# Routed blocks of 512 rows chosen after six batches, two shared tiles moved to the end, and a re-ordered opening

## The chip, the cores and the metric

One Trainium2 chip, one NeuronCore. The metric is the device time of one execution in microseconds; the median of 3 runs of the kernel before is 559.57 us (558.17 to 560.89). TensorE (PE) multiplies, VectorE (DVE), ScalarE (ACT) and GpSimd (POOL) work on elements, SyncE (SP) issues most DMAs. Each engine works through its own list of instructions in the order written, and semaphores order the engines among each other.

## What is computed

Eight batches of 512 tokens with 256 features, in float32: a pre-norm attention with one head and a causal mask, and then a pre-norm mixture of experts with one shared and eight routed experts, of which each token takes two.

```python
x = x + attn(layernorm(x), Wq, Wk, Wv)          # x: 8 x 512 x 256, causal, softmax(q k / 16)
h = layernorm(x)
shared = (silu(h @ sg.T) * (h @ su.T)) @ sd.T    # inner size 512
probs = sigmoid(h @ router.T + bias)             # 8 experts
scores, idx = top_k(probs, 2); scores /= scores.sum()
x = x + shared + sum over the two of scores * (silu(h @ gate[e]) * (h @ up[e])) @ down[e]
```

## The kernel before, in words

**Products.** Every operand is split into a float16 high and a low part, and each product is made of three passes, hi x hi, lo x hi and hi x lo (`PASSES`), summed in PSUM.

**First stage, attention.** The kernel goes through the eight batches. For each: statistics, normalising (`xn_normalise`, `xn_high`, `xn_low`), transposing by DMA, T = x (Wq Wk^T) and V products, scores, softmax, a DMA transpose of the probabilities, and PV; then the second norm, the logits, `route` and `weights` (the two experts of each token), `prefix` and `places` (the place of each token in the list of its expert), and `scatter`, which writes each token's normalised row and its scores to the lists in `rows` in HBM, one list of T + P rows for each expert. Batch 0 is transposed by TensorE instead (`first_transposes`, `first_xn_high`, `first_xn_low`).

The weights of the nine experts come in 36 pieces of 384 KB through two buffers: `w_load(g)` on SP (it waits for `w_low(g - 2)`), `w_scale(g)` and `w_high(g)` on ACT, `w_low(g)` on POOL, which counts up `w_lo`.

The shared expert is done in 16 tiles of 256 tokens (`SHARED`), two batches behind the attention: `shared_gate_up(t, half)` on TensorE; `tanh`, `split_h` on ACT and `ffn_gate`, `ffn_up`, `ffn_low` on DVE make the hidden values h; `shared_down(t)` multiplies them into the bank Y, and `add_shared(t)` on DVE adds Y to x1, the sum so far. A tile's half takes 24 matmuls of 256 columns, and so does its `down`. `gate_up` of the next tile's same half waits for `f_h` (gate and up have been read), `shared_down` for `f_lo` (h is complete) and for `y_read` (Y has been added), and the weight loads, the norms and this work share the queues in an order written out by hand. `out_base(b)` writes x1 of a batch to `out`.

**Second stage, routed experts.** The lists are cut into pieces by tables that DVE works out from the counts: 26 pieces of 256 rows ("pairs"), of which the first 18 are two halves of 9 blocks of 512 rows (`QUADS`, `table_of_quads`), 12 of 128 ("singles") and 7 of 64 ("halves"). `counts()` on TensorE sums the tokens of each expert over all eight batches, `cnt_mm` tells DVE, and `tab`, `tab2` and `tab3` tell the other engines that a table is written. Each step of a table is a small DVE operation on one partition. SP then reads row numbers into registers (`value_load`) and loads the rows with a transposing DMA (`load_pair_rows`, `load_single_rows`) and the scores (`load_pair_aux`). A pair runs like a shared tile, with the expert's number from a register; then ACT scales its result by the scores (`y_copy`) and POOL adds it to `out` in HBM, 128 rows at a time (`y_add`, `add_rows`), one addition at a time. All lists' first 128 rows are filled with padding at the start (`zero_rows`), and a piece may reach down into them.

**Around the stages.** TensorE ends the first stage with `shared_down(15)`, waits for `tab` and for all 36 weight pieces, and starts the first groups: pair 0, then (after `tab2`) single 0, pair 1, and so on. SP loads the first pairs only when all batches are scattered. The last group is pairs 24 and 25, its last half in chunks (`last_gate_up`, `down_parts`), so that the last addition starts early; the kernel ends with POOL's last addition.

## Time and profile before

| what | value |
|---|---|
| median of 3 runs | 559.57 us (558.17 to 560.89) |
| the profiled execution, first to last instruction | 555.3 us |
| TensorE busy | 518.0 us (93%), 4757 matmuls |
| DVE, ACT, POOL busy | 369.8 (67%), 301.0 (54%), 288.9 us (52%) |
| mean granted TensorE clock | 0.986 of full |
| DMA | 68.55 MB, mean 123 GB/s |

The busy share of TensorE is a share of time in which a matmul was under way; what counts for the end is where it was not, and what it then waited for. Start times and durations below are those of the profiled execution, in us from its first instruction. An operation's line is often that of a helper, so operations are told apart by tile and time. "xN" groups N like instructions that follow each other.

### The profile page before, as it was taken

What the parts mean: (1) busy time and instruction counts of PE and PEld (TensorE: products, weight loads), DVE (VectorE), ACT (ScalarE), POOL (GpSimd) and SP (SyncE); (2) the same over time, 40 slices, a digit from 0 to 9 for tenths busy, and PEclk for the clock granted to TensorE, in tenths of its full rate; (3) what the DMA queues carried; (4) which work ended last, traced back from release to release, by engine and by line L of the source; (5) the groups of instructions that cost most, each with busy time, mean ns of one, the idle gap of its engine ahead of it and who ended that gap; (6) DMA issues with size and microseconds to landing.
All of it is one profiled execution on the core that took longest, in us unless ns stands there. A gap on an engine that the chain in (4) does not pass through costs nothing.

```text
span 555.3 us, 14903 instructions
## 1 busy us (share of the span) xinstructions
PE 518.0 (93%) x4757; PEld 425.5 (77%) x4757; DVE 369.8 (67%) x980; ACT 301.0 (54%) x580; POOL 288.9 (52%) x242
## 2 busy tenths in 40 slices
PE   4889988999999999997999999999999999999992
PEld 3557766788878888886767788888787888888881
DVE  5788998689887878899747555445454454454551
ACT  3989877678777676744233443433343433434341
POOL 4466677668676765857022344452444434434443
PEclk9999999899999999998899999999999999999998
DMA  8799848949694947414465965764846536345443
GB/s 271 201 181 208 178 127 158 217 133 209 161 208 141 194 127 170 155 70 136 131 115 85 98 107 69 103 83 60 108 59 89 73 60 97 55 65 78 62 58 38
DMA packets 139351, 68.55 MB, mean 123 GB/s; under 512 B 114608, under 2 KB 132336, under 8 KB 139280
## 3 DMA queue, kind: packets, MB, share of 16 engines
q1 hardware_dynamic: 126128, 48.84, 43.5%
q0 software_dynamic: 13152, 18.76, 19.4%
q8 instruction: 44, 0.72, 0.5%
q14 instruction: 27, 0.22, 0.1%
HBM read 19.46 MB, written 23.08 MB: 77 GB/s over the span
## 4 chain that ended last, share of the span: by engine, by line
PE 65%; DVE 12%; DMA 8%; SPq 5%; ACT 5%; issue 3%; POOL 1%; POOLq 0%; ACTq 0%; DVEq 0%
PE bank L2216 29%; PE bank L2240 15%; PE bank L2547 4%; PE bank L2322 3%; PE bank L2564 3%; DMA v<-xnrow 2%; PE bank L2625 2%; PE bank L2347 2%; PE bank L2392 2%; DMA xn2t<-xrow 2%; PE bank L2369 2%; PE bank L2640 2%; SPq L405 2%; DMA x<-x 1%; DVE h L1470 1%
## 5 line engine op out<-in xcount | busy, mean ns | idle before, releaser
L2216 PE MATMUL bank<-xn2t,w 128*128 128x256 f16 x1608 | 184.9, 273 | 1.3 <-DVE th L1653 1.1
L2216 PEld LDWEIGHTS bank<-xn2t,w 128*128 (+1 forms) x1608 | 155.2, 98 | 24.3 <-DVE th L1653 2.2
L1644 DVE SCALAR_TENSOR_TENSOR th<-th,bank 128x512 f32<-128x512 f32 x83 | 56.6, 682 | 55.2 <-ACT th L989 54.1
L2240 PE MATMUL bank<-w,h 128*128 (+1 forms) x768 | 91.5, 273 | 0.0
L943 ACT ACTIVATE h<-th 128x512 f16<-128x512 f32 (+1 forms) x69 | 42.9, 622 | 84.6 <-DVE th L1653 78.3
L989 ACT ACTIVATE th<-bank 128x512 f32<-128x512 f32 x83 | 49.2, 593 | 62.1 <-PE bank L2216 47.6
L2240 PEld LDWEIGHTS bank<-w,h 128*128 128x128 f16 x768 | 74.0, 98 | 10.4 <-DVE x L1676 0.3
L866 POOL DMA_INDIRECT out<-p,wm x28 | 43.9, 1569 | 67.2 <-ACT p L1323 27.3
L1470 DVE TENSOR_TENSOR h<-th,h 128x512 f16<-128x512 f32 (+1 forms) x69 | 50.6, 733 | 38.3 <-ACT h L943 38.1
L734 POOL TENSOR_TENSOR w<-wst,w 128x768 f16<-128x768 f32 x36 | 59.1, 1645 | 18.9 <-ACT w L943 18.7
L758 POOL DMA_INDIRECT rows<-xrow,sidx x56 | 56.5, 1009 | 17.0 <-issue 13.3
L866 POOL DMA_INDIRECT out<-phl,wm x24 | 38.1, 1587 | 39.1 <-DMA out<-tt,wm 13.0
L1653 DVE SCALAR_TENSOR_TENSOR th<-th,bank 128x512 f32<-128x512 f32 x83 | 56.8, 684 | 2.0
L866 POOL DMA_INDIRECT out<-tt,wm x12 | 19.7, 1644 | 41.0 <-DMA out<-x 17.2
L2216 PE MATMUL bank<-w 128*128 128x256 f16 x288 | 34.5, 280 | 0.0
L2547 PE MATMUL bank<-w,ptr 128*128 x144 | 33.0, 379 | 0.4 <-DMA ptr<-rows 0.4
L943 ACT ACTIVATE xnrow<-xn 128x512 f16<-128x512 f32 (+2 forms) x26 | 17.8, 684 | 26.1 <-DVE xn L2107 17.4
L2216 PEld LDWEIGHTS bank<-w 128*128 128x128 f16 x288 | 28.4, 100 | 4.2
L2322 PE MATMUL bank<-v,ptr 128*128 128x256 f16 x240 | 29.7, 273 | 1.2 <-DMA ptr<-phl 1.0
L943 ACT ACTIVATE wst<-wst 128x768 f32<-128x768 f32 x36 | 30.1, 836 | 0.6 <-DMA wst<-w_all 0.6
L943 ACT ACTIVATE w<-wst 128x768 f16<-128x768 f32 x36 | 30.1, 840 | 0.5
L704 POOL TENSOR_TENSOR rstd<-ve,halves 128x4 f32<-128x4 f32 x16 | 16.9, 1058 | 25.5 <-DVE ve L1490 23.0
(188 smaller groups left out, 808.4 us busy)
## 6 DMA issues: line engine op xcount, KB each, us to landing
wst<-w_all SPq DMA_DIRECT2D x36, 384.0 KB
x<-x SPq DMA_DIRECT2D x8, 512.0 KB, 5.6
out<-x SPq DMA_DIRECT2D x8, 512.0 KB, 4.0
rows<-xrow POOLq DMA_DIRECT2D x1, 1192.5 KB, 6.6
rows<-xrow,sidx POOLq DMA_INDIRECT x56
out<-p,wm POOLq DMA_INDIRECT x28
xn2t<-rows SPq DMA_TRANSPOSE x26
wm<-rows SPq DMA_DIRECT2D x26, 9.0 KB, 2.4
```

The source lines that it names most:

```text
L734: cc.tensor_tensor(w_ap(j, 1, c * CH, CH), wst[:, (g % 2) * CH:(g % 2 + 1) * CH], w_ap(j, 0, c * CH, CH), ALU.subtract).then_inc(w_lo, 1)
L758: cc.indirect_dma_start(rows, bass.IndirectOffsetOnAxis(ap=sidx_of(b)[:, m:m + 1], axis=0), xrow[b % 2][:, n * RW:(n + 1) * RW].bitcast(I3 ...
L866: cc.indirect_dma_start(out, bass.IndirectOffsetOnAxis(ap=index, axis=0), part, None, compute_op=ALU.add).then_inc(y_out, 16)
L943: return a.activation(o, i, ACT.Copy, scale=scale)
L989: a.activation(th[:, half * 512:(half + 1) * 512], G[half][:, :], ACT.Tanh, scale=0.5 / WS).then_inc(f_tanh, 1)
L1470: return d.tensor_tensor(o, full, hi, ALU.subtract)
L1644: d.scalar_tensor_tensor(out=tb, in0=tb, scalar=1.0, in1=G[half][:, :], op0=ALU.add, op1=ALU.mult).then_inc(f_sg, 1)
L1653: d.scalar_tensor_tensor(out=tb, in0=tb, scalar=0.5 / (WS * WS), in1=U[half][:, :], op0=ALU.mult, op1=ALU.mult).then_inc(f_h, 1)
L2216: ins = mm(dst, w_ap(j, ws, m * MAT + k * I + (2 * half + i) * P, P), moving(ms * KD + k), start=(cnt == 0), stop=(cnt == 3 * KD - 1))
L2240: ins = mm(o[:, a * D:(a + 1) * D], hb[:, (hs * KI + i) * TT + a * P:(hs * KI + i) * TT + (a + 1) * P], w_ap(j, ws, 2 * MAT + i * D, D), s ...
L2322: ins = mm(PV_BANK[q // 2][:, (q % 2) * D:(q % 2 + 1) * D], ptr[:, off + (ps * (q + 1) + kb) * P:off + (ps * (q + 1) + kb + 1) * P], v[:, ...
L2547: ins = mm(o[:, :], xs_t[:, c * P:(c + 1) * P], w_ap(j, ws, m * MAT + kk * I, I), start=(cnt == 0), stop=(cnt == 3 * KD - 1))
```

## The change

It is made of three parts.

**Opening.** `first_transposes` runs by column block, each into a bank of its own (`X0_BANK`), and ACT copies a block when it is there. `first_t_product` does the passes with the high part of x first and those with its low part last. `wm_low` comes before `stats_1(2)` on DVE; `w_scale(0)`, `w_scale(1)` and `w_high(0)`, `w_high(1)` come later on ACT, and `w_load(2)`, `w_load(3)` later on SP.

**Early blocks.** `counts_seen()` counts after six batches (`SEEN`), `table_of_quads` makes 5 blocks of 512 rows (`QUADS`) from that, and pairs 0 to 3 of these run (`plain_groups`) in place of the last two shared tiles, with the norm, transposes, logits, routing and `counts()` of batch 7 between them. Then one chain of 56 steps on DVE (`tab2`) makes the tables of the other 16 pairs, of the singles and of the halves, with the halves of pair 3's hidden values between. The lists now start at 0 and are filled at the end: `zero_ends()` on SP reads eight row numbers and copies 128 rows of padding behind each list, in HBM, and `rows_complete()` waits for that and for all scatters. The last weight loads, `w_load(34)` and `w_load(35)`, are issued behind the rows of pair 0; `w_scale` and `w_high` of pieces 29 to 35 stand at other places in ACT's list, and `w_low` and the scatters of batch 6 and 7 in POOL's.

**End.** The last two shared tiles (`LATE`) run behind pair 25. SP writes batch 7's x1 to `out` before they are added, waits for all additions (`ALL_ADDS`), reads both tiles back, DVE adds the shared results, and SP writes them with plain DMAs. The last tile's two halves go to banks of their own (`last_down`).

```diff
-MORE = PAIRS - 2 * QUADS
-EARLY = 2 * (QUADS - 1)
+SEEN = 6
+QUADS = -(-(SEEN * S * TOPK - E * (2 * TT - 1)) // (2 * TT))
+EARLY = 2 * QUADS
+MORE = PAIRS - EARLY
...
             p_transpose(0, 0)
             x_load(4)
             p_transpose(0, 1)
+            w_load(2)
             p_transpose(0, 2)
             p_transpose(0, 3)
+            w_load(3)
...
             p_transpose(7, 3)
             w_load(31)
             w_load(32)
+            out_base(4)
             w_load(33)
-            out_base(4)
-            w_load(34)
-            w_load(35)
...
+            def zero_ends():
+
+                for e in range(E):
+                    end = sp.value_load(end_tab[0:1, e:e + 1], min_val=0, max_val=ROWS - P)
+                    sp.dma_start(rows[ds(end, P), :], rows[SPARE:SPARE + P, :]).then_inc(pads_in, 16)
+
+            def rows_complete():
+
+                sp.wait_ge(rows_in[0], scattered(B - 2))
+                sp.wait_ge(rows_in[1], scattered(B - 1))
+                sp.wait_ge(pads_in, 16 * E)
...
 
             sp.wait_ge(tab, T_STEPS)
             pair0, pair1 = pair_row(0), pair_row(1)
             sp.wait_ge(rows_zero, 16)
-            sp.wait_ge(rows_in[0], scattered(B - 2))
-            sp.wait_ge(rows_in[1], scattered(B - 1))
-            load_pair_rows(pair0, 0, 2 * SHARED - 4)
-            load_pair_rows(pair1, 1, 2 * SHARED - 4)
+            sp.wait_ge(rows_in[0], scattered(SEEN - 2))
+            sp.wait_ge(rows_in[1], scattered(SEEN - 1))
+            load_pair_rows(pair0, 0, 2 * AHEAD - 2)
+            w_load(34)
+            w_load(35)
+            load_pair_rows(pair1, 1, 2 * AHEAD)
             load_pair_aux(pair0, 0, 0, 0)
+            load_pair_aux(pair1, 1, 0, 0)
+            out_base(5)
+            out_base(7)
+            out_base(6)
+            pair_rows(2)
+            pair_aux(2)
+            pair_rows(3)
+            pair_aux(3)
+            pair_rows(4)
             sp.wait_ge(tab2, T2_STEPS)
-            single0, single1 = single_row(0), single_row(1)
-            load_single_rows(single0, 0, 0)
-            load_single_rows(single1, 1, 0)
-            load_single_aux(single0, 0, 0, 0)
-            out_base(5)
-            out_base(6)
-            out_base(7)
+            zero_ends()
...
-            for i in range(2, GROUPS - 1):
+            for i in range(PLAIN + 2, GROUPS):
                 group(i)
-            n = PAIRS - 1
-            load_pair_aux(pair_row(n), n % 4, 16 * (n // 4), after("pair", n - 4))
             sp.wait_ge(y_out, ALL_ADDS)
+
+            def tile_rows(t):
+                return out[t * TT:(t + 1) * TT, :].rearrange("(n p) d -> p n d", p=P)
+
+            def tile_of(t):
+                return x1[:, 2 * t * D:2 * (t + 1) * D].rearrange("p (n d) -> p n d", n=2)
+
+            for i in range(LATE):
+                sp.dma_start(tile_of(AHEAD + i), tile_rows(AHEAD + i)).then_inc(back_in[i], 16)
+            sp.wait_ge(y_read, AHEAD + PAIRS + 1)
+            sp.dma_start(tile_rows(AHEAD), tile_of(AHEAD)).then_inc(out_done, 16)
+            for a in range(2):
+                n = 2 * (SHARED - 1) + a
+                sp.wait_ge(z_put, a + 1)
...
             scatter(5, 1, 4)
+            table_iota()
             w_low(29)
             scatter(5, 4, 5)
             w_low(30)
             scatter(5, 5, 8)
             last_identity()
+            w_low(31)
+            w_low(32)
+            scatter(6, 0, 1)
+            w_low(33)
+            scatter(6, 1, 2)
+            w_low(34)
+            scatter(6, 2, 3)
+            w_low(35)
+            scatter(6, 3, 5)
             rstd2(7)
-            table_iota()
             put_idx(7)
...
+            scatter(6, 5, 8)
...
+            w_high(29)
             tanh(11, 0)
             split_h(10, 1)
+            w_scale(30)
             logits_exp(6)
-            w_high(29)
-            w_scale(30)
+            w_high(30)
             tanh(11, 1)
             split_h(11, 0)
-            w_high(30)
+            w_scale(31)
+            w_high(31)
             split_h(11, 1)
-            w_scale(31)
+            w_scale(32)
+            w_high(32)
             tanh(12, 0)
-            w_high(31)
+            w_scale(33)
+            w_high(33)
             tanh(12, 1)
-            xn2_normalise(7, 0)
-            xn2_high(7, 0)
             split_h(12, 0)
-            xn2_normalise(7, 1)
-            xn2_high(7, 1)
-            split_h(12, 1)
...
-            tanh(15, 1)
-            split_h(15, 0)
-            split_h(15, 1)
             w_scale(34)
             w_high(34)
+            tanh(13, 0)
+            split_h(12, 1)
             w_scale(35)
             w_high(35)
+            split_h(13, 0)
+            tanh(13, 1)
+            split_h(13, 1)
 
...
-                used(c, PREV_P, MORE, FOURS)
-                less_used(c, TWOS, TWOS, 2)
-                less_used(c, LEFT, LEFT, 4)
-                less_used(c, BASE, BASE_P, TT); c.last()
-                c.then(d.tensor_scalar(BASE, BASE, float(TT - P), None, ALU.add))
+                                              in1=TWOS[:, E - 1:E], op0=ALU.is_ge, op1=ALU.add)); c.last()
+                plus_used(c, TWOS, TWOS, USED_Q, -4)
+                sums_before(c, FOURS, INC, PREV)
+                table(c, MORE, 1, EARLY, TT, INC, PREV, BASE)
+                used(c, USED, PREV, MORE, FOURS)
+                return c.k
...
             aggregate_1(1)
+            wm_low()
+            first_xn_low(1)
+            shift_1(1)
+            first_xn_low(0)
+            wv_low()
+            router_low()
             stats_1(2)
-            wm_low()
...
             ffn_low(11, 1)
             ffn_gate(12, 0)
+            ffn_up(12, 0)
+            ffn_gate(12, 1)
+            ffn_up(12, 1)
+            add_shared(10)
+            table_of_quads()
+            ffn_low(12, 0)
+            ffn_gate(13, 0)
+            ffn_low(12, 1)
+            add_shared(11)
+            ffn_up(13, 0)
+            stats_2(7)
+            ffn_gate(13, 1)
+            aggregate_2(7)
+            ffn_low(13, 0)
+            ffn_up(13, 1)
+            add_shared(12)
+            ffn_low(13, 1)
             shift_2(7)
-            ffn_up(12, 0)
-            add_shared(10)
-            ffn_gate(12, 1)
-            row_numbers(6)
-            last_xn2_low(0)
...
+            def plain_groups():
+
+                t = AHEAD
+                ffn_half(t, 0)
+                add_shared(13)
+                ffn_low(t, 0)
+                last_xn2_low(0)
+                ffn_half(t, 1)
+                last_xn2_low(1)
+                ffn_low(t, 1)
+                ffn_half(t + 1, 0)
+                last_xn2_t_low(1)
+                last_xn2_t_low(0)
+                ffn_low(t + 1, 0)
+                ffn_half(t + 1, 1)
+                read_logits(7)
+                ffn_low(t + 1, 1)
+                route(7)
+                ffn(t + 2, 0)
+                weights(7)
+                places(7)
+                row_numbers(7)
+                ffn(t + 2, 1)
+                k = table_of_pairs()
+                ffn(t + 3, 0)
+                k = table_of_singles(k)
+                ffn(t + 3, 1)
+                table_of_halves(k)
...
+            def last_group():
+
+                t = AHEAD + PAIRS
+                ffn(t, 0)
+                ffn(t, 1)
+                ffn(t + 1, 0)
+                ffn(t + 1, 1)
+                dve.wait_ge(back_in[0], 16)
+                dve.wait_ge(dn_mm, t * 2 + 2)
+                o = x1[:, 2 * AHEAD * D:2 * (AHEAD + 1) * D]
+                d.scalar_tensor_tensor(out=o, in0=Y[:, :], scalar=1.0 / WS, in1=o, op0=ALU.mult,
+                                       op1=ALU.add).then_inc(y_read, 1)
+                dve.wait_ge(back_in[1], 16)
+                for a in range(2):
+                    n = 2 * (SHARED - 1) + a
+                    o = x1[:, n * D:(n + 1) * D]
+                    dve.wait_ge(z_mm, a + 1)
+                    d.scalar_tensor_tensor(out=o, in0=PARTS[a][:, 0:D], scalar=1.0 / WS, in1=o, op0=ALU.mult,
+                                           op1=ALU.add).then_inc(z_put, 1)
...
+                    ws, ms = PASSES[p]
+                    return mm(T_BANK[m][:, :].rearrange("p (n r) -> p n r", r=P),
+                              wm[:, (ws * KD + k) * D + m * P:(ws * KD + k) * D + (m + 1) * P],
+                              xn4(0)[:, :, ms * KD + k, :], start=(k == KD - 1 and p == 0),
+                              stop=(k == 0 and p == 1))
+
+                pe.wait_ge(wm_lo, 1)
+                for i, k in enumerate((1, 0)):
+                    pe.wait_ge(xn0_hi, i + 1)
+                    for p in (0, 2):
+                        for m in range(KD):
+                            part(m, k, p)
+                for i, k in enumerate((1, 0)):
+                    pe.wait_ge(xn0_lo, i + 1)
+                    for m in range(KD):
+                        ins = part(m, k, 1)
+                        if k == 0:
...
+            def counts_seen():
+
+                pe.wait_ge(p_lo, NB * (B - 1) + 2)
+                pe.wait_ge(px_dve, 3 * SEEN - 1)
+                mm(PT0[:, 2 * NB * E:2 * NB * E + E], ones[:, :], cumh[:, :], start=True, stop=True).then_inc(cnt_mm, 1)
...
+            def plain_groups():
+
+                pair_gate_up(0, 0)
+                shared_down(13, 0, 2)
+                expert(1)
+                pair_gate_up(0, 1)
+                last_transposes(0)
+                last_transposes(1)
+                pair_gate_up(1, 0)
+                expert(2)
+                pair_down(0)
+                pair_gate_up(1, 1)
+                logits(7)
+                pair_gate_up(2, 0)
+                expert(3)
+                pair_down(1)
+                pair_gate_up(2, 1)
+                prefix(7)
+                pair_gate_up(3, 0)
+                expert(4)
+                pair_down(2)
+                counts()
+                pair_gate_up(3, 1)
+
             def first_groups():
...
-                gate_up(t, 0, expert(0), pair_moving(0), False)
-                expert(1)
-                gate_up(t, 1, expert(0), pair_moving(0), False)
+                p = 2 * PLAIN
+                pair_gate_up(p, 0)
...
+                t = AHEAD + PAIRS
+                gate_up(t, 0, 0, half_batch(xn24(B - 1), 0), True)
+                pair_down(PAIRS - 1)
+                gate_up(t, 1, 0, half_batch(xn24(B - 1), 0), True)
+                gate_up(t + 1, 0, 0, half_batch(xn24(B - 1), 1), True)
+                gate_up(t + 1, 1, 0, half_batch(xn24(B - 1), 1), True)
+                down(t, 0)
+                last_down()
+
             pe.wait_ge(tab, T_STEPS)
             pe.wait_ge(w_lo, (E + 1) * CHUNKS)
+            plain_groups()
             first_groups()
```

## Rows read from the trace of the kernel before

**Rows 1.** Windows: stretch, us, busy us of each engine (instructions), clock, DMA share, GB/s.
```profile
20.00:40.00 20.00, 18.35 (x137) 12.05 (x135) 16.17 (x51) 17.63 (x42) 10.62 (x9) 1.00 0.94 202
40.00:60.00 20.00, 17.93 (x169) 13.85 (x170) 17.66 (x64) 19.32 (x39) 15.55 (x13) 1.00 0.84 183
80.00:100.00 20.00, 15.11 (x151) 12.19 (x149) 16.40 (x51) 12.20 (x28) 12.52 (x11) 0.99 0.79 145
258.00:261.00 3.00, 0.00 (x0) 0.00 (x0) 2.87 (x6) 2.28 (x4) 0.96 (x1) 0.83 0.25 93
261.00:267.00 6.00, 5.90 (x29) 4.26 (x30) 5.59 (x24) 1.90 (x3) 3.26 (x2) 0.52 0.45 89
```

**Rows 2.** TensorE's waits, 220 to 310: for whom, total us, times, longest.
```profile
PE bank L2240 <- DVE x L1676: 3.1, 1, 3.1
```

**Rows 3.** Timeline of TensorE: start us, us, engine, line, out<-in, count [idle before].
```profile
249.69 2.79 PE L2240 MATMUL bank<-w,p 128*128 128x256 f16 x24
252.31 2.78 PE L2216 MATMUL bank<-xnt,w 128*128 128x256 f16 x24
```

**Rows 4.** Timeline of the opening: T product and first scores of batch 0.
```profile
15.55 2.76 PE L2347 MATMUL bank<-xnt,wm 128*128 128x512 f16 x12 [3.30 <-DVE xnt L1470]
...
21.29 0.51 PE L2392 MATMUL bank<-xnt,tt 128*128 128x128 f16 x6 [0.35 <-DVE tt L1470]
```

**Rows 5.** Timeline at 250 us: an `ffn_low` on DVE and two `w_low` on POOL.
```profile
250.37 4.12 DVE L1470 TENSOR_TENSOR h<-th,h 128x512 f16<-128x512 f32 x1
...
250.69 3.24 POOL L734 TENSOR_TENSOR w<-wst,w 128x768 f16<-128x768 f32 x2
```

**Rows 6.** Timeline at 225 us: a `w_scale`, batch 5's last scatter, `gate_up(13,0)`.
```profile
222.45 0.83 ACT L943 ACTIVATE wst<-wst 128x768 f32<-128x768 f32 x1
...
224.51 0.96 POOL L758 DMA_INDIRECT rows<-xrow,sidx  x1 [0.30 <-issue]
...
228.73 2.79 PE L2216 MATMUL bank<-xn2t,w 128*128 128x256 f16 x24
```

**Rows 7.** The page's DMA issues: count, KB each, median us to landing.
```profile
x<-x SPq DMA_DIRECT2D x8, 512.0 KB, 5.6
out<-x SPq DMA_DIRECT2D x8, 512.0 KB, 4.0
...
wm<-rows SPq DMA_DIRECT2D x26, 9.0 KB, 2.4
```

**Rows 8.** Timeline of DVE: first and last of the 20 steps of `table_of_quads`.
```profile
245.56 0.07 DVE L1790 MEMSET phl<- 1x8 f32 x1
...
248.38 0.17 DVE L1774 TENSOR_SCALAR start_tab<-phl 1x18 int32<-1x18 f32 x1
```

**Rows 9.** From `tab2` to single 0: SP's chain (two register reads, transpose), timeline.
```profile
268.24 0.27 SPq L521
...
268.81 0.26 SPq L521
...
269.47 1.48 SPq L542
...
272.33 2.76 PE L2547 MATMUL bank<-w,ptr 128*128 x12 [0.44 <-DMA ptr<-rows]
272.48 0.43 SPq L550 DMA_DIRECT2D wm<-rows  x1
```

**Rows 10.** Timeline of DVE: a half tile from gate (first) to low (last).
```profile
297.31 0.67 DVE L1644 SCALAR_TENSOR_TENSOR th<-th,bank 128x512 f32<-128x512 f32 x1
...
299.40 0.69 DVE L1470 TENSOR_TENSOR h<-th,h 128x512 f16<-128x512 f32 x1 [0.69 <-ACT h L943]
```

**Rows 11.** The end: an addition's landing (chain of waits), last matmuls, last addition (timeline).
```profile
542.11 3.70 DMA out<-p,wm
...
543.31 1.72 PE L2689 MATMUL bank<-w,h 128*128 x12 [0.48 <-DVE h L1470]
...
547.99 1.56 POOL L866 DMA_INDIRECT out<-p,wm  x1 [0.30 <-issue]
```

770 lines of the change are left out of this document (344 added, 426 removed).

## Prediction, made before the changed kernel was run

> **What bounds the kernel now.** I read the page's first two sections, then the table of windows, then the waits of TensorE, and then the timelines around its longest waits. TensorE is busy for 93% of the span, and nearly all of what is missing lies in four places: the opening, the stretch up to 100 us, the change from shared to routed experts, and the end [rows 1, 4, 11]. Between 100 and 540 us it hardly waits, so there a microsecond is won or lost only by what makes TensorE wait. The one long wait of the change of stage is 3.1 us for a shared add [rows 2]. It stands in the window that shows no matmul at all; in the 6 us behind it the granted clock is 0.52, about the lower of its two levels (1.2 GHz of 2.4) [rows 1]. So that wait costs 3.0 us and about 2.9 us more (0.48 of 6): 5.9 us. The edit leaves the matmuls as they are but for one of 8 columns, so it can only move waits.
>
> The unit of TensorE time below: 24 matmuls of 256 columns (one half of a tile's gate and up, or one tile's down) start 2.62 us after the 24 before them [rows 3].
>
> **The opening.** The wait for the first operands stays. Then TensorE waits 3.3 us for both low parts of the first transposed block; the first T product starts at 15.55 and the first scores at 21.29 [rows 4]. After the change the hi passes need only the hi copy and `wm_low`, which moves ahead of one group of statistics, and the two weight scalings leave ACT until the first softmax. T starts about 3 us earlier, and the scores about as much, since ACT (normalise, `xn_high`, two copies) then sets them. But from 20 to 60 us ACT is busy 17.6 and 19.3 of each 20 us and the DMA engines 0.94 and 0.84 [rows 1], and there the moved scalings and loads come back. I take -2 us; bounds -4 (the whole lead, with less queueing for the probability transposes) and 0.
>
> **Into the routed experts, first chain.** What goes: the 5.9 us above. It came of DVE: an `ffn_low` took 4.12 us beside two `w_low` of GpSimd [rows 5] and made all later ones late; the last `w_low`s now stand elsewhere.
> What comes: tile 13's TensorE work now waits for ACT operations that stand behind weight loads in ACT's queue. In before's clock: GpSimd ends its scatters of batch 5 at 225.47 [rows 6]; the new order brings `w_high(30)` forward, so about 223.4. The identity (0.7) and `w_low(31)` (half of 3.24 [rows 5]) follow, to 225.8, and only then can SP issue `w_load(33)`. It lands in some 3.4 us (512 KB take 4.0, 9 KB 2.4 [rows 7]); `w_scale` and `w_high` take 0.83 each [rows 6], so `tanh(12,1)`, queued behind them, ends at 231.5, gate and up at 232.8, `add_shared(10)` at 233.5. TensorE has done `down(10)` and `gate_up(13,0)` by 231.4 [rows 3, 6] and waits 2.1 us for the bank Y. Then 2 units, to 238.8.
> `table_of_quads` follows on DVE: 18 steps; before, 20 took 3.0 us [rows 8], so 2.8 us, to 236.3. SP waits for it, reads two registers (0.57 us each), issues a transpose (1.4 us) [rows 9], and only behind that stands `w_load(34)`: issued 238.8, landed 242.4. On ACT `tanh(13,0)` and `split_h(12,1)` are queued behind `w_scale(34)` and `w_high(34)` (244.1); they end at 245.3, `ffn_low(12,1)` at 246.0, `add_shared(11)` at 246.7, and `shared_down(12)` needs it. TensorE waits from 238.8: 7.9 us. Together +10.0 us. Bounds: +4 if `w_load(33)` hides and a load lands in 2.4 us; +13 if loads queue behind the transpose and take the 5.6 us of an x load [rows 7]. A gap that long should be followed by the lower clock as before: +2.9 (0 to 3).
> Beside it the last two `w_low` run while DVE does `ffn_low(12,1)` and `ffn_low(13,0)`. The trace shows that such a pair can hold DVE: 4.12 us against 0.69 [rows 5, 10]; elsewhere DVE and GpSimd run side by side unharmed. I take nothing for it, and 3.4 us as its upper bound.
> The Trainium skill ("SBUF — State Buffer", on what makes engines contend) makes this a rule: a VectorE instruction with two SBUF inputs and a GpSimd instruction that reads SBUF exclude each other for the whole instruction. The row agrees, and by that rule the sum would have 3.4 us more.
>
> **The first plain pairs.** Pair 0 to 3 need no count of batch 7, so its transposes, logits, routing and scatters go beside them. DVE now has the routing (some 3 us) ahead of a half tile, so `down(2)` should wait for its low part: +1.5 (0 to 4).
>
> **Second chain: counts to first single.** This decides. Call the moment of the matmul of `counts()` zero. TensorE then has `gate_up(3,1)`, `gate_up(4,0)`, `down(3)` and `gate_up(4,1)`: 4 units, 10.5 us, until it wants single 0. The way to single 0 is serial:
> DVE: 26 steps for pairs, a half tile, 16 steps for singles, a half tile, 14 steps for halves. At 0.15 us a step [rows 8] that is 3.9, 2.4 and 2.1. A half tile from gate to low is 2.8 us (tables hold it back, and it the tables) [rows 10]. Sum 14.0 us.
> SP: it waits for `tab2`, then `zero_ends()` reads a register and issues a copy in HBM eight times: 0.57 and 0.43 (a DIRECT2D issue) each [rows 9]: 8.0 us. `rows_complete()` waits for the last to land: 2.4 us for 9 KB [rows 7], 2.7 taken for 135 KB. A register and the transpose up to the matmul that waits: 0.57 + 2.9 (269.47 to 272.33 [rows 9]). Sum 14.2 us.
> 28.2 us against 10.5: TensorE stands for 17.7 us, in parts (`gate_up(4,0)` and `down(3)` for DVE, `single_gate_up(0)` for SP). Behind the waiting SP stand single 1 and the rows of pair 5: two more transposes with registers, 3.9 us, less the single's 2.6 us of work and plus the longer landing: +2 (0 to 4). Clock behind it +2.9 (0 to 5, there being several gaps). Bounds of the main term: +12 if the half tiles fall wholly into TensorE's work and the copies issue in 0.8 us each, +24 if landings take 5 us.
> The batch 7 scatters hide: eight of 0.96 us and two adds of GpSimd, with `row_numbers(7)` some 4 us ahead of `counts()`, should be done before SP has got through the copies.
>
> **The end.** Now the last matmul ends at 545.03 and the span at 555.3: 10.3 us with two adds by GpSimd in a row, of which the last lands at 551.7 (547.99 + 3.70), and 3.6 us of ending [rows 11]. After the change: DVE's add 0.5, a plain write of 128 KB about 2.8 (between 2.4 and 4.0 [rows 7]), and the same 3.6: 7.0. Gain 3 us. The adds and the read-back are covered by 5 units, 13.1 us, against 0.8 (copy) + 3.4 (two descriptor runs) + 3.7 (landing) + 4.0 (the read-back, at most) = 11.9; if GpSimd is behind, 1 to 3 us of it go. Bounds -4.5 and 0.
>
> **Sum**, in the profiled execution: 555.3 - 2 - 5.9 + 10.0 + 2.9 + 1.5 + 17.7 + 2 + 2.9 - 3 = 581.4. The median of the runs, 559.57, is 4.3 us above the span, so 585.7. All low bounds give 561 (555.3 - 4 - 5.9 + 4 + 12 - 4.5 = 556.9, + 4.3), all high ones (with the DVE hold) 610.
>
> **Rivals.**
> 1. Faster: the chains fit under TensorE's work. Mechanism: between `counts()` and `single_gate_up(0)` 10.5 us cover all. It decides from a chain of 10.5 us down; for that the 56 steps would have to overlap the half tiles and the eight copies issue nearly at once. For it: DVE's part alone (14.0 us) is not far above the cover. Against: each register read stands in the chain of SP at 0.57 us [rows 9]. Time: 555.3 - 2 - 5.9 + 1.5 - 3 + 4.3 = 550.2. Chance 0.15.
> 2. The first chain hides (`w_load(33)` and `w_load(34)` land in time), the second does not: 585.7 - 10.0 - 2.9 = 572.8. For it: tile 13's weights could be asked for early, there being two buffers; against: `w_load(34)` stands behind the wait for `tab`. Chance 0.10.
> 3. DVE is held by the `w_low`s besides: 585.7 + 3.4 = 589.1. For it [rows 5], against it the many pairs that run unharmed. Chance 0.10. (The Trainium skill, "SBUF — State Buffer", states this as a rule, see above.)
> 4. It doesn't do what it says: single 0 is reached late for both reasons at their low bounds, and the gains of opening and end just pay for it: 561, within 0.5% of before. Chance 0.04.
> Forecast 0.61.
>
> **Numbers.** 585.7 us. Range 563 to 601: it leaves out rival 1 and the ends. A measurement of this kernel can tell about 0.5%. Faster 0.15, within 0.5% 0.04, slower 0.81.
>
> **What would show it.** In the profile after: a TensorE wait of 2 us before `shared_down(11)` and some 8 us before `shared_down(12)`, both for the shared add on DVE; then waits for `th` of pair 3 and for `h` of pair 3; and one of over 10 us at the first single, ended by the DMA that loads its rows, with SP issuing eight copies in the 8 us before it; clock near 0.5 behind the long gaps; the last matmul 7 us before the end. Wrong it is if those eight copies cost under 3 us, if `tab2` is complete before `gate_up(4,0)`, or if `tanh(13,0)` starts within a few us of its matmuls.

## The result: 24.5 us slower

| | before | after |
|---|---|---|
| median of the runs | 559.05 us (558.17 to 560.89, 4 runs) | 583.57 us (582.41 to 585.70, 4 runs) |
| span of the profiled execution | 555.3 us | 584.0 us |
| from the last matmul's end to the span's end | 10.3 us | 9.0 us |

The ratio is 1.0435, 95% interval 1.039 to 1.048. The prediction was 585.7 us, range 563 to 601. The profiled execution of the changed kernel belongs to its slowest run (585.70 us), so the two spans lie 28.7 us apart where the medians lie 24.5.

The page's row of granted clock shows where to look: it dips at 240 to 260 us and at 290 to 320 us. TensorE's waits over the whole span (for whom, total us, times, longest), the three that are new or have grown:

```profile
PE bank L2624 <- DMA ptr<-rows: 14.4, 1, 14.4
PE bank L2326 <- issue: 9.3, 2, 9.1
...
PE bank L2279 <- DVE th L1706: 5.0, 3, 3.5
```

Windows (columns as in [rows 1]):

```profile
240.00:250.00 10.00, 0.93 (x9) 0.57 (x8) 2.65 (x4) 4.26 (x6) 2.88 (x2) 0.71 0.57 133
...
290.00:300.00 10.00, 6.89 (x36) 4.88 (x36) 7.75 (x31) 2.96 (x6) 8.17 (x7) 0.66 0.50 94
...
310.00:320.00 10.00, 1.43 (x4) 0.66 (x5) 0.00 (x0) 0.00 (x0) 0.00 (x0) 0.50 0.43 94
```

Before had one such hole, of 3 us [rows 1, 2]. Now there are two, 240 to 250 and 304 to 319. In the second, from 310 until single 0 starts at 318.57, no engine but SyncE does anything.

**First chain**, the timeline of all engines (start us, us, engine, line, operation, count, idle before and its releaser):

```profile
227.93 0.33 SPq L393 DMA_DIRECT2D wst<-w_all  x1
229.30 0.22 DVE L1689 TENSOR_REDUCE sidx<-pm 128x8 int32<-128x64 f32 x1 [1.31 <-DMA rows<-xrow,sidx]
231.03 0.84 ACT L998 ACTIVATE wst<-wst 128x768 f32<-128x768 f32 x1 [0.23 <-DMA wst<-w_all]
232.31 2.79 PE L2279 MATMUL bank<-xn2t,w 128*128 128x256 f16 x24 [1.30 <-DVE th L1706]
239.63 1.28 SPq L538 DMA_TRANSPOSE xn2t<-rows  x1
240.96 1.04 SPq L393 DMA_DIRECT2D wst<-w_all  x2
245.12 0.84 ACT L998 ACTIVATE wst<-wst 128x768 f32<-128x768 f32 x1 [11.37 <-DMA wst<-w_all]
247.22 0.62 ACT L998 ACTIVATE h<-th 128x512 f16<-128x512 f32 x1
247.96 1.15 DVE L1521 TENSOR_TENSOR h<-th,h 128x512 f16<-128x512 f32 x1
249.03 0.68 DVE L1729 SCALAR_TENSOR_TENSOR x<-bank,x 128x512 f32<-128x512 f32 x1
249.81 5.02 PE L2326 MATMUL bank<-w,h 128*128 128x256 f16 x24 [9.07 <-issue]
```

Read it from the bottom. `shared_down(12)` waits 9.07 us. The trace names no releaser ("issue"), but `add_shared(11)` on VectorE (249.03) ends 0.10 us before its start and the low part of `ffn_low(12,1)` (247.96) 0.7 us before; it needs both, and the add stands behind the low part in VectorE's list. The low part needs `split_h(12,1)`, which is ScalarE's row at 247.22. That stands behind `w_scale(34)` at 245.12, where ScalarE has been idle for 11.37 us for the load of piece 34. SyncE issued that load at 240.96, behind the transpose of pair 0 at 239.63, and that one waited for the first table. The 24 matmuls of `shared_down(12)` then take 5.02 us where they take 2.8 in [rows 3].

**Second chain**, the same view:

```profile
286.76 0.17 PE L2520 MATMUL bank<-cumh,ones 128*128 128x8 f16 x1
287.07 0.15 DVE L1864 TENSOR_SCALAR x<-bank 1x8 int32<-1x8 f32 x1 [1.74 <-PE bank L2520]
293.06 5.30 PE L2279 MATMUL bank<-xn2t,w 128*128 128x256 f16 x24 [3.48 <-DVE th L1706]
302.23 0.16 DVE L1827 TENSOR_SCALAR start_tab<-x 1x7 int32<-1x7 f32 x1
303.15 10.02 SPq L615 DMA_DIRECT2D rows<-rows  x8
315.70 3.12 SPq L553 DMA_TRANSPOSE ptr<-rows  x2
318.57 4.78 PE L2624 MATMUL bank<-w,ptr 128*128 x12 [14.35 <-DMA ptr<-rows]
```

`counts()` at 286.76, tables on VectorE from 287.07 to 302.39, eight copies on SyncE from 303.15 to 313.17, the transpose at 315.70, single 0 at 318.57: one thing after the other, with TensorE's four units (of 24 matmuls each) finished at 304.2.

**The end** (timeline):

```profile
562.13 0.84 ACT L1364 ACTIVATE p<-bank,wm 128x256 f32<-128x256 f32 x2
571.29 1.55 POOL L925 DMA_INDIRECT out<-p,wm  x1 [3.10 <-DMA out<-p,wm]
572.25 2.78 PE L2800 MATMUL bank<-w,v 128*128 128x256 f16 x24
573.15 1.71 POOL L925 DMA_INDIRECT out<-p,wm  x1 [0.30 <-issue]
577.08 0.89 SPq L706 DMA_DIRECT2D x<-out  x2
579.89 0.69 DVE L2227 SCALAR_TENSOR_TENSOR x<-bank,x 128x512 f32<-128x512 f32 x1 [6.47 <-DMA x<-out]
580.61 0.38 SPq L708 DMA_DIRECT2D out<-x  x1
```

The last matmul ends at 575.03, and the span 9.0 us later (before: 10.3 us, [rows 11] and the span). The last pair's product was copied by 562.97, but GpSimd adds it only at 571.29, behind the landing of the pair before it. The read-back waits for the landing of that last addition.

### The profile page after: what moved, and what is told of

It reads as the page before. It is cut to its first block, busy times and chain, and to the rows that moved or that the text cites. A ratio compares the mean times of both kernels' runs of the same rounds, so it can differ in the third digit from the quotient of the medians.

```text
span 584.0 us, 14963 instructions
## 1 busy us (share of the span) xinstructions
PE 521.9 (89%) x4758; PEld 428.0 (73%) x4758; DVE 366.4 (63%) x978; ACT 301.9 (52%) x578; POOL 292.1 (50%) x242
## 4 chain that ended last, share of the span: by engine, by line
DMA 32%; PE 26%; issue 14%; DVE 8%; SPq 6%; POOL 6%; ACT 5%; POOLq 0%; DVEq 0%; ACTq 0%
PE bank L2279 9%; DMA out<-p,wm 8%; PE bank L2326 7%; DMA out<-phl,wm 6%; DMA out<-tt,wm 6%; DMA out<-x 4%; SPq L415 3%; DMA wst<-w_all 3%; PE bank L2624 3%; POOL out L925 2%; PE bank L2408 2%; PE bank L2429 2%; DMA w<-xrow 2%; POOL w L797 1%; DMA x<-x 1%
## 5 line engine op out<-in xcount | busy, mean ns | idle before, releaser
L2279 PE MATMUL bank<-xn2t,w 128*128 128x256 f16 x1632 | 190.6, 275 | 5.0 <-DVE th L1706 5.0
L2279 PEld LDWEIGHTS bank<-xn2t,w 128*128 (+1 forms) x1632 | 158.9, 99 | 27.8 <-issue 3.8
L2326 PE MATMUL bank<-w,h 128*128 (+1 forms) x816 | 100.1, 277 | 10.0 <-issue 9.3
L1697 DVE SCALAR_TENSOR_TENSOR th<-th,bank 128x512 f32<-128x512 f32 x84 | 57.4, 683 | 67.7 <-ACT th L1044 66.8
L2326 PEld LDWEIGHTS bank<-w,h 128*128 128x128 f16 x816 | 80.1, 100 | 23.2 <-issue 12.0
L998 ACT ACTIVATE h<-th 128x512 f16<-128x512 f32 x68 | 42.7, 628 | 96.5 <-DVE th L1706 90.9
L1521 DVE TENSOR_TENSOR h<-th,h 128x512 f16<-128x512 f32 x68 | 47.9, 704 | 37.8 <-ACT h L998 37.6
L821 POOL DMA_INDIRECT rows<-xrow,sidx x56 | 58.9, 1052 | 14.4 <-issue 12.9
L925 POOL DMA_INDIRECT out<-phl,wm x24 | 38.7, 1612 | 41.7 <-DMA out<-tt,wm 15.2
L1706 DVE SCALAR_TENSOR_TENSOR th<-th,bank 128x512 f32<-128x512 f32 x84 | 57.5, 685 | 2.1
L2624 PE MATMUL bank<-w,ptr 128*128 x144 | 35.1, 396 | 14.6 <-DMA ptr<-rows 14.4
L925 POOL DMA_INDIRECT out<-tt,wm x12 | 19.6, 1630 | 38.7 <-DMA out<-x 13.1
L2624 PEld LDWEIGHTS bank<-w,ptr 128*128 128x128 f16 x144 | 14.6, 101 | 30.9 <-issue 17.6
## 6 DMA issues: line engine op xcount, KB each, us to landing
rows<-rows SPq DMA_DIRECT2D x8, 132.5 KB, 2.6
```

Of the source, the lines that this page charges most:

```text
L821: cc.indirect_dma_start(rows, bass.IndirectOffsetOnAxis(ap=sidx_of(b)[:, m:m + 1], axis=0), xrow[b % 2][:, n * RW:(n + 1) * RW].bitcast(I3 ...
L925: cc.indirect_dma_start(out, bass.IndirectOffsetOnAxis(ap=index, axis=0), part, None, compute_op=ALU.add).then_inc(y_out, 16)
L998: return a.activation(o, i, ACT.Copy, scale=scale)
L1521: return d.tensor_tensor(o, full, hi, ALU.subtract)
L1697: d.scalar_tensor_tensor(out=tb, in0=tb, scalar=1.0, in1=G[half][:, :], op0=ALU.add, op1=ALU.mult).then_inc(f_sg, 1)
L1706: d.scalar_tensor_tensor(out=tb, in0=tb, scalar=0.5 / (WS * WS), in1=U[half][:, :], op0=ALU.mult, op1=ALU.mult).then_inc(f_h, 1)
```

## The experiments

All ratios are to the kernel before, run beside each kernel on the same chip, with 95% intervals. The column of microseconds is ratio times 559.05, so that all kernels stand on one scale; a difference below about 3 us between two rows is within the intervals (below 5 us where w34_early, both_early or warm is one of them).

| kernel | ratio | interval | us on one scale |
|---|---|---|---|
| changed kernel | 1.0435 | 1.039 to 1.048 | 583.4 |
| w34_early | 1.0235 | 1.016 to 1.031 | 572.2 |
| ends_early | 1.0261 | 1.021 to 1.031 | 573.6 |
| both_early | 1.0101 | 1.004 to 1.016 | 564.7 |
| tables_last | 1.0467 | 1.040 to 1.053 | 585.2 |
| open_only | 1.0014 | 0.998 to 1.005 | 559.8 |
| open_mid | 1.0019 | 0.998 to 1.006 | 560.1 |
| no_readback | 1.0358 | 1.031 to 1.041 | 579.1 |
| cover | 1.0298 | 1.025 to 1.035 | 575.7 |
| rows5 | 1.0073 | 1.004 to 1.011 | 563.1 |
| half_first | 1.0083 | 1.005 to 1.012 | 563.7 |
| warm | 1.0377 | 1.032 to 1.043 | 580.1 |
| rows5_warm | 1.0037 | 1.001 to 1.007 | 561.1 |

### w34_early: the weight loads ahead of the wait for the table

```diff
             w_load(33)
+            w_load(34)
+            w_load(35)
...
             load_pair_rows(pair0, 0, 2 * AHEAD - 2)
-            w_load(34)
-            w_load(35)
```

> The changed kernel, with the loads of the last two weight chunks (34 and 35) issued right behind the load of chunk 33, ahead of SyncE's wait for the first table. Theory (the first long wait is the chain table, pair 0's rows, load of chunk 34, ScalarE's w_scale(34), split_h(12,1)): the 11.4 us that ScalarE waited for that load go, shared_down(12) starts at about 240.8 where it started at 249.8, and the 24 matmuls after it take 2.8 us and not 5.0. Time: 583.6 - 9.1 - 2.2 = 572.3, range 571 to 576. Rival (the table and pair 0's rows are late by themselves, SyncE waits for them whatever stands behind): shared_down(12) goes forward, but pair 0's gate_up then waits for its rows till about 249, and the time is 580 to 584.

Measured: 11.2 us less than the changed kernel, where 11.3 were expected. Timeline of TensorE:

```profile
243.45 2.78 PE L2326 MATMUL bank<-w,h 128*128 128x256 f16 x24 [2.23 <-issue]
...
312.20 5.25 PE L2624 MATMUL bank<-w,ptr 128*128 x12 [14.54 <-DMA ptr<-rows]
```

The wait of 9.07 us is one of 2.23, the product takes 2.78 us, and single 0 waits as long as before (14.54 against 14.35). A little is given back further on: from `counts()` to single 0 it is 33.6 us (278.57 to 312.20) and no longer 31.8, and 1.7 of these 1.8 us lie ahead of VectorE's first step of the tables, which comes 2.02 us behind `counts()` and not 0.31. The trace names no source for that signal. The first chain was two loads standing behind a wait that they had nothing to do with.

### ends_early: the eight copies beside the tables

```diff
+            sp.wait_ge(tab2, 2)
+            zero_ends()
             sp.wait_ge(tab2, T2_STEPS)
-            zero_ends()
             rows_complete()
```

> The changed kernel, with the eight copies of zero_ends issued as soon as the experts' ends are in their table (the second step of the second table's chain, about 287.2) and no longer after its last step (302.4). Theory (single 0 waits for tables and copies one after the other, 1.3 us a copy): the copies end at about 298, single 0's rows are read from 302.5 on and its matmuls start at about 306 instead of 318.6: 12.5 us, and up to 2 us more because TensorE stands still for under 2 us instead of 14.4 and its clock stays up. Time 583.6 - 14 = 569.6, range 568 to 573. Rival (something other than the copies holds single 0: the last scatters, the adds of the early pairs on the same queue, or single 0's scores): no more than 5 us are gained, 579 to 584.

Measured: 9.8 us less, between the two expectations. Timeline of SyncE and TensorE:

```profile
288.94 15.41 SPq L615 DMA_DIRECT2D rows<-rows  x8
...
308.20 3.76 SPq L553 DMA_TRANSPOSE ptr<-rows  x2
```
```profile
294.64 4.02 PE L2280 MATMUL bank<-xn2t,w 128*128 128x256 f16 x20 [4.79 <-DVE th L1707]
...
301.08 0.38 PE L2280 MATMUL bank<-xn2t,w 128*128 128x256 f16 x2 [1.14 <-issue]
...
311.16 2.76 PE L2625 MATMUL bank<-w,ptr 128*128 x12 [0.29 <-DMA ptr<-rows]
...
316.57 2.79 PE L2280 MATMUL bank<-xn2t,w 128*128 128x256 f16 x24 [2.65 <-DMA xn2t<-rows]
```
```profile
298.88 0.25 DVE L1824 TENSOR_TENSOR x<-x 1x96 f32<-1x96 f32 x1 [1.23 <-DVE w_tab L1823]
```

Single 0 hardly waits any more (0.29 us), so the copies behind the tables were indeed its last link. It starts at 311.16 where 306 was expected, since the tables, which now come last, end at 307.51: they take 19.9 us from their first step and not 15.3, because VectorE's small steps stand apart by up to 1.2 us (the row at 298.88). The copies are slower too, 15.4 us (1.9 each) where they had taken 10.0 (1.25 each), but have been issued by 304.35. Batch 7's scatters and the adds of the early pairs run beside them; that this is the reason is not shown, for rows5 below has the same beside its copies, and they take 10.1 us. TensorE pauses in this stretch as well (the row at 301.08); cover below has more of this. Other waits came up besides: 4.8 us ahead of `gate_up(4,0)` (3.5 before), and 2.65 for pair 5's rows, which both kernels load behind single 1's.

### both_early: both edits

> Both edits at once. Theory (two separate chains, one after the other, nothing shared): the gains add up, 583.6 - 11.3 - 14 = 558.3, range 557 to 564, about the kernel before. Rival (what is gained at the first is given back at the second, since the tables wait for batch 7's counts, which hang on the attention and not on the shared tiles): 566 to 572.

Measured: 18.7 us less than the changed kernel; the sum of the two is 21.0, which the intervals allow, but 564.7 is 6 us above what was expected and lies between the two expectations; 4 of the 6 us are what ends_early was short of. In its profile the waits are these:

```profile
287.64 4.48 PE L2280 MATMUL bank<-xn2t,w 128*128 128x256 f16 x23 [5.86 <-issue]
...
297.25 1.85 PE L2327 MATMUL bank<-w,h 128*128 x12 [2.82 <-DVE h L1522]
...
308.45 4.43 PE L2280 MATMUL bank<-xn2t,w 128*128 128x256 f16 x24 [2.66 <-DMA xn2t<-rows]
```

So two places of SyncE's program, neither of which touches what is computed, hold three quarters of the loss (18.7 of 24.5 us).

### tables_last: the three tables behind pair 3's halves

```diff
-                k = table_of_pairs()
                 ffn(t + 3, 0)
-                k = table_of_singles(k)
                 ffn(t + 3, 1)
+                k = table_of_pairs()
+                k = table_of_singles(k)
                 table_of_halves(k)
```

> The changed kernel, with VectorE's three tables after pair 3's two halves and not in between. Theory (the wait of 3.5 us ahead of gate_up(4,0) is no cost of its own, since single 0's rows come last in any case): that wait goes, the wait ahead of single 0 grows from 14.4 to about 17, the tables end within 1 us of 302.4, and the time is 583.6 within 1.5. Rival (what VectorE's tables cost is that they stand between the halves): 583.6 - 3.5 - 2.5 of slow clock = 577.6, range 576 to 580.

Measured: 1.8 us more than the changed kernel, not different within the intervals, and not the rival's 6 us less. The wait ahead of `gate_up(4,0)` is gone and single 0's grew by more than it:

```profile
288.25 0.38 PE L2279 MATMUL bank<-xn2t,w 128*128 128x256 f16 x2 [0.41 <-issue]
...
322.57 4.42 PE L2624 MATMUL bank<-w,ptr 128*128 x12 [21.40 <-DMA ptr<-rows]
```

The tables were expected within 1 us of where they were, and they end 22.2 us behind `counts()` (284.15 to 306.34) where the changed kernel takes 15.6. Part of that are pauses of which the first row shows the beginning: the second half of pair 3, which now stands ahead of the tables, reaches VectorE only at 294.14. cover below has them too.

### The opening alone: open_only and open_mid

open_only is the kernel before with every hunk of the diff that belongs to the opening (transposes and T product, and the new places on all five engines). open_mid puts three of these places back:

```diff
             router_low()
             stats_1(2)
+            aggregate_1(2)
+            shift_1(2)
             t_low(0, 0)
...
             v_high(0, 0)
+            xn_normalise(2)
             w_scale(0)
...
+            xn_high(2)
             p_high(0, 3)
```

> The kernel before with the opening of the change alone (transposes by column block, T product by passes, and the new places of the loads, of the weight splits and of block 2's normalising on all engines). Theory (the opening loses more by its new places than it gains by its passes: in the changed kernel the first scores start 1.75 us earlier, but gate_up(12,0) 2.3 us later): 2.3 us slower than the kernel before, ratio 1.004, range 1.001 to 1.008. Rival (the prediction's term: 2 us gained, and what the changed kernel lost by 222 us came from elsewhere): ratio 0.996, range 0.993 to 1.000.

> The same opening, but block 2's statistics, xn_normalise(2) and xn_high(2) where the kernel before has them: on VectorE ahead of t_low(0,0), on ScalarE ahead of exp_of(0,0) and p_high(0,3). Theory (it is block 2's late normalising, 6 us later in the changed kernel, that costs the waits for xnt behind it): the 1.75 us lead is kept, the wait for the transposed xnt of block 2 goes, and the time is 1 to 3 us under open_only, ratio to the kernel before 0.996 to 1.000. Rival (the loss comes from the loads of the weights, which this one leaves where the change puts them): as open_only within 1 us.

Measured: 0.8 us and 1.1 us more than the kernel before, neither different from it. The expected 2.3 us lie inside open_only's interval and the predicted gain of 2 us (ratio 0.996) outside it: the opening brings nothing, and whether it costs can't be told. Its profile shows the lead and how it goes (timeline of TensorE):

```profile
14.32 2.76 PE L2237 MATMUL bank<-xnt,wm 128*128 128x512 f16 x12 [2.12 <-DVE wm L1472]
...
20.02 0.51 PE L2412 MATMUL bank<-xnt,tt 128*128 128x128 f16 x6 [0.32 <-DVE tt L1471]
```
```profile
37.73 2.57 PE L2367 MATMUL bank<-xnt,wm 128*128 128x512 f16 x6 [2.10 <-DMA xnt<-xnrow]
```

The T product starts 1.23 us earlier than in [rows 4] and the first scores 1.27; 18 us later the T product of a following block waits 2.10 us for its transposed rows. In the kernel before there is no wait for those. open_mid was to remove that wait and did not: it still shows 2.7 us of it, and 3.1 us ahead of the first score besides, which starts at 22.82, where [rows 4] has 21.29. So block 2's late place is not shown to be the cause, and open_mid, which loses the lead itself, is no clean test of it; which of the moved loads and copies is the cause stays open.

### no_readback: the end without the read-back

The last two tiles are not read back from the output (these 512 rows lack their experts' part), VectorE adds to what is in SBUF:

```diff
-            for i in range(LATE):
-                sp.dma_start(tile_of(AHEAD + i), tile_rows(AHEAD + i)).then_inc(back_in[i], 16)
...
-                dve.wait_ge(back_in[0], 16)
+                dve.wait_ge(out_done, 16 * B)
...
-                dve.wait_ge(back_in[1], 16)
```

> The changed kernel without the two loads that read tiles 14 and 15 back at the end (these 512 rows of the output lack their experts' part): VectorE adds the shared expert's product to the tile in SBUF at once, and the stores still wait for the last adds. Theory (the end is the chain last pair's adds, read-back, VectorE, store): VectorE is done at about 576.5 instead of 581, the stores leave at 577.1 instead of 580.6, and the time is 3.5 us lower, 580.1, range 579 to 581.5. Rival (the last matmuls and the landing of the adds alone set the end): within 1 us of the changed kernel.

Measured: 4.3 us less, where 3.5 were expected; the rival falls. The store of the first tile is issued 0.1 us after VectorE's add, and no longer 3.5 us behind the landing of the last pair's adds. The span ends 2.7 us behind the last matmul, not 9.0; not all of these 6.3 us are the read-back's, since GpSimd was less far behind in this execution (4.1 us from the copy of the last product to its adds, against 8.3). Timeline:

```profile
576.54 0.68 DVE L2225 SCALAR_TENSOR_TENSOR x<-bank,x 128x512 f32<-128x512 f32 x1
577.31 0.39 SPq L706 DMA_DIRECT2D out<-x  x1
```

### cover, rows5 and half_first: what is left of the second chain

```diff
+            pair_rows(5)                      # rows5
             sp.wait_ge(tab2, 2)
             zero_ends()
...
             single_rows(1)
-            pair_rows(5)                      # rows5
...
+                ffn(t + 3, 0)                 # half_first
                 k = table_of_pairs()
-                ffn(t + 3, 0)                 # half_first
```

All three are both_early with one or both of these: rows5, half_first, and cover with both.

> The changed kernel with both edits of both_early, pair 5's rows loaded ahead of the eight copies and not behind single 1's, and VectorE's half 0 of pair 3 ahead of the table of pairs. both_early still shows 5.9 us of wait ahead of gate_up(4,0), 2.8 ahead of its half down product, 2.7 for pair 5's rows, and three products of 4.1 to 4.5 us at the lower clock. Theory (each of these waits is an order on one engine, and the low clock hangs on them): the 5.9 and the 2.7 go, single 0 may wait 1 to 2 us more for tables that start 2 us later, and two of the three slow products take 2.8 us: 8.6 + 3 - 2 = 9.6 us under both_early, ratio to the kernel before 0.993, range 0.988 to 1.003. Rival (the tables set the time of single 0, and everything waits there instead): within 2 us of both_early, ratio 1.007 to 1.012.

> both_early with pair 5's rows ahead of the eight copies, nothing else (one of cover's two additions). Theory (pair 5's rows wait on SyncE's queue only because they stand behind the copies): the 2.7 us for pair 5's rows go, ratio to the kernel before 1.005 (both_early 1.010), range 1.001 to 1.009. Rival (it is this one that made cover slower: the transposes take the place of the copies, all eight start later and single 0 waits): 1.015 to 1.025.

> both_early with VectorE's half 0 of pair 3 ahead of the table of pairs, nothing else (cover's other addition). Theory (cover was slower because of this one: gate_up(4,0) starts without a wait and is then issued two matmuls at a time, with pauses of 0.37 us, for some 8 us, and the tables end later): ratio 1.02 to 1.03 and the pauses are seen again. Rival (the pauses were one run's accident): no pauses, ratio 1.000 to 1.008.

Measured: cover is 11 us slower than both_early, against both of its expectations. Each half alone is not slower (1.6 and 1.0 us less than both_early, within the intervals), so the expectation that named half_first as the cause is wrong too. What cover's profile shows:

```profile
281.10 0.38 PE L2280 MATMUL bank<-xn2t,w 128*128 128x256 f16 x2 [0.37 <-issue]
281.86 0.38 PE L2280 MATMUL bank<-xn2t,w 128*128 128x256 f16 x2 [0.38 <-issue]
...
288.52 0.60 ACT L1045 ACTIVATE th<-bank 128x512 f32<-128x512 f32 x1 [10.06 <-remote]
```

From 279.6 to 286.9 TensorE goes two matmuls at a time, with some 0.37 us of nothing between them, and the trace names no releaser for them. ScalarE is idle for 10 us there (remote: the signal that ended it has no source in the trace). It waits for `gate_up(3,1)`, and so does SyncE's transpose of pair 5's rows, which is issued at 288.67 only; yet that product began at 275.53 and, at its usual 2.8 us, was over at 278.3, ten us before either moves. The transpose stands ahead of the copies in cover, so they start at 290.73, 15.2 us behind `counts()`, where rows5 has 5.0. This is how the late signal becomes late copies, read from the order of the program and not tested by itself. rows5 and half_first have no such pauses, although half_first too starts `gate_up(4,0)` without a wait; tables_last has them over 7 us, and ends_early has two. All four runs of cover took long (574.07 to 579.56 us beside a median of 560.67 of the kernel before), so its loss is no accident of one execution. What makes the pauses is open: the trace has no row for it.

### warm and rows5_warm: what the clock costs

```diff
+            keep_busy(PT1, 70)
             shared_down(12, 0, 2)
...
                 pe.wait_ge(tab2, T2_STEPS)
+                keep_busy(GS, 110)
                 single_gate_up(0, 0, 16)
...
+            def keep_busy(o, n):
+                for _ in range(n):
+                    mm(o[:, 0:TT], w_ap(0, 0, 0, P), w_ap(0, 0, 0, TT), start=True, stop=True)
```

rows5_warm is rows5 with 15, 25 and 25 such matmuls in its three remaining waits.

> The changed kernel with matmuls that nobody reads put into its two long waits: 70 ahead of shared_down(12) (8.1 us of the 9.1) and 110 ahead of single 0's gate_up (12.8 us of the 14.4), each into a PSUM bank that is next overwritten. No wait gets shorter. Theory (the waits cost TensorE's clock besides their length: the 24 matmuls behind the first take 5.0 us and not 2.8, the 12 behind the second 4.8 and not 2.8): the granted clock stays at 1.0 behind both, and the time is 2.2 + 2.0 = 4.2 us lower, 579.4, range 578 to 581. The prediction has 2.9 for each, 5.8 in all: 577.8. Rival (what stands behind the waits is bound by other things, so that the low clock costs nothing): 583 to 584.

> rows5 with matmuls that nobody reads in the waits that it still has: 15 ahead of shared_down(12), 25 ahead of gate_up(4,0) (2.9 us of its 3.5) and 25 ahead of single 0's gate_up (2.9 of 3.6). Theory (what is left of the second chain is half length, half clock): the 24 matmuls of gate_up(4,0) take 2.8 us instead of 5.3, single 0's 12 take 2.8 instead of 4.4, 4.1 us less than rows5 and about as fast as the kernel before: ratio 1.000, range 0.996 to 1.004. Rival (short waits leave no slow clock that counts, or the added matmuls stand in the way): as rows5, 1.005 to 1.010.

Measured: warm is 3.3 us below the changed kernel, with intervals as wide as that; rows5_warm 2.0 us below rows5, less than the 4.1 expected, and for that pair the intervals overlap too. The profile is clearer than the times. warm, TensorE:

```profile
246.80 2.78 PE L2326 MATMUL bank<-w,h 128*128 128x256 f16 x24 [1.86 <-issue]
...
314.23 2.76 PE L2630 MATMUL bank<-w,ptr 128*128 x12 [2.31 <-DMA ptr<-rows]
...
318.53 2.79 PE L2279 MATMUL bank<-xn2t,w 128*128 128x256 f16 x24 [1.54 <-DMA xn2t<-rows]
```
```profile
310.00:320.00 10.00, 6.14 (x44) 3.96 (x42) 1.61 (x3) 1.23 (x2) 0.00 (x0) 1.00 0.28 54
```

The same two products as in the changed kernel, 2.78 and 2.76 us instead of 5.02 and 4.78, at a granted clock of 1.00: 4.3 us of matmul time that hung on nothing but TensorE's having stood still ahead of them. Not all of it reaches the end of the kernel: behind the faster single 0, TensorE waits 1.54 us for pair 5's rows (the row at 318.53), which had landed under the slow one. In rows5_warm too the two products take 2.8 us, but the second half of `down(3)` then waits 2.73 us where it waited 0.32, and TensorE reaches single 0 22.3 us behind `counts()` and not 21.0. rows5_warm, with the waits of both chains shortened or filled, is the fastest form of the change that was measured, and its interval (1.001 to 1.007) still lies above the kernel before.

## Why the prediction was right

The place, the mechanism and the size held; single terms were off in both directions. That the number came within 2.1 us is partly luck: the span was predicted at 581.4 and was 584.0, and the 4.3 us added to get from the span to the median of the runs, taken from the kernel before, are -0.4 here. Predicted terms against the two profiles:

| step | predicted | profile |
|---|---|---|
| opening | -2 | +2.3 |
| before's wait and its clock gone | -5.9 | -5.9 |
| ahead of and inside tile 13 | +10.0 | +10.6 (1.30 + 0.23 + 9.07) |
| clock behind it | +2.9 | +2.2 (5.02 - 2.78) |
| plain pairs | +1.5 | +0.5 |
| counts to single 0 | +17.7 | +18.0 (3.48 + 0.18 + 14.35) |
| pair 5's rows | +2 | 0 |
| clock behind it | +2.9 | +4.5 (5.30 - 2.78, 4.78 - 2.78) |
| end | -3 | -1.3 |
| sum | +26.1 | +30.9 |

The spans differ by 28.7, so that the right column has 2.2 us too many; they were not traced.

**Opening: wrong in sign in the profile.** `gate_up(13,0)` without its wait starts at 231.01 against 228.73 in [rows 6]: 2.3 us late. The step that failed is "T starts about 3 us earlier, and the scores about as much": the T product started at 13.84 and the scores at 19.54, so the lead was 1.7 us and not 3, and it was given back between 20 and 47 us; at 60 us the changed kernel is 1.6 us behind. The prediction saw the place where it would be (the busy windows of [rows 1]) and took too little for it. By the runs of open_only it lies between 1 us gained and 2.6 us lost.

**First chain: right link by link.** `w_load(33)` landed in 3.1 us, `w_scale(34)` waited for a load behind the transposed rows, `shared_down(12)` waited 9.07 us where 7.9 were worked out. w34_early shows the cause by taking it away. Of the 2.1 us for the bank Y only 0.23 came there; 1.30 came earlier, for `th` of tile 12, by a path that the prediction does not have. `tanh(12,0)` at 230.21 did not stand in ScalarE's queue (ScalarE had been idle for 2.70 us); it waited for `ffn_low(11,0)` on VectorE, and that stands behind `row_numbers(6)`, which waits for batch 5's scatters to have landed (the row at 229.30). The prediction followed these scatters only to `w_load(33)`. The price of the load (3.4 us) was nearly right; the load of 34 took 4 us to the row at 245.12.

**VectorE held by `w_low` (rival 3): hardly.** The low part at 247.96 takes 1.15 us instead of 0.69 beside the `w_low` of 246.93, 0.5 us and not 3.4; the two `w_low` do not come back to back as in [rows 5]. Earlier, at 226.37, the multiplication of `row_numbers(6)` takes 1.61 us beside two `w_low`, where the other batches' take 0.22; what follows waits for the scatters in any case, until 229.30, so this hold cost nothing there. w34_early, both_early and rows5 show a stronger case, in rows5:

```profile
232.56 1.71 DVE L1853 CAST x<-x 1x8 f32<-1x8 int32 x1
232.59 1.65 POOL L798 TENSOR_TENSOR w<-wst,w 128x768 f16<-128x768 f32 x1
```

A cast of eight numbers, 0.16 us in the changed kernel, ends with GpSimd's operation (234.27 and 234.24). The Trainium skill ("SBUF — State Buffer", "SBUF: two separate sides") has the exclusive lock also for VectorE instructions with one SBUF input, where they run in a two-port mode; the two rows fit that, though they don't show the mode.

**Plain pairs and pair 5's rows: too dear.** The routing on VectorE hid but for 0.5 us. Pair 5's rows landed while single 0 was at work, at the lower clock; with the clock kept up, in warm, TensorE waits 1.54 us for them. So of this term and the clock term behind it one covers a part of the other, and they were added.

**Second chain: the sum right, its parts not.** The tables took 15.5 us (286.9 to 302.39) where 14.0 were predicted, and SyncE's part 16.2 (to 318.57) where 14.2 were: a copy with its register read costs 1.25 us and not 1.0. Against that stands a cover of 13.8 us and not 10.5, since the four units ran partly at the lower clock. They also waited 3.7 us inside. So the wait for single 0 was 14.35, and with those 3.7 the total is 18.0.

**Clock: a little short for the second chain.** There are two holes in it, ahead of `gate_up(4,0)` and ahead of single 0, and each has a slow product behind it. With the wait filled, the one behind single 0's takes 2.76 us (warm), and the one behind `gate_up(4,0)`'s 2.79 (rows5_warm).

**End: the named risk came.** The prediction covers the read-back with 13.1 us against 11.9, "if GpSimd is behind, 1 to 3 us of it go". It was behind by a whole pair: the copy of the last product is done at 562.97, the add starts at 571.29. The backlog is an older one: the adds of a pair take 6.5 us with the landing (564.75 to 571.29) and the products come every 7.9 us (copied from 538.55, 546.41, 554.27 and 562.13 on), so GpSimd was catching up, from 12.3 us behind to 9.2, and did not get there. By the runs of no_readback the read-back costs 4.3 us.

**Rivals.** Rival 1 (all covered) needed a chain of 10.5 us; it was 31.8 (286.76 to 318.57). Rival 2 (the first chain hides) is roughly what w34_early makes of the kernel: 572.2 against its 572.8, though 2.12 and 2.23 us of waits are left in that chain. Rival 4 named low bounds; pair 5's rows came to theirs (0) and the plain pairs near theirs, but neither of the two large terms did. None of the three signs of being wrong showed: the copies took 10.0 us, `tab2` was complete 9.3 us behind the start of `gate_up(4,0)`, and `tanh(13,0)` (246.74) came 11.6 us behind the end of its matmuls (235.10).

## What to carry to other kernels

Before moving work earlier, follow every queue that the move passes through: here two weight loads stood behind a wait for a table and eight copies behind another, and moving these few lines gave back 18.7 of the 24.5 us. Price a wait at its length plus the slow matmuls behind it, less what those slow matmuls cover, and when one link of a serial chain is taken out, look for the next late one before adding up gains. Starting an opening step a microsecond or two earlier brought nothing here: the lead was gone within 30 us, while ScalarE and the DMA engines behind it were busy nearly all the time.
